# Graph network kernel, adjacency build: one 128-partition store of counts per window, or four stores of 32 partitions sent off an epoch apart

## What is computed

```python
edge_index = jnp.stack([src, dst])
h = jnp.maximum(_layernorm(x, axis=-1), 0.0)
x = x + _L0_gnn_ref(h, edge_index, ...)          # aggr = segment_sum(x[src], dst)
h = jnp.maximum(_layernorm(x, axis=-1), 0.0)
x = x + _L1_gnn_ref(h, ..., src, dst)            # the same sums, divided by the degree
...                                              # two further layers, untouched
```

## Time and profile before

| | us |
|---|---|
| median of 3 runs | 3777.47 |
| lowest, highest | 3775.76, 3778.92 |
| the profiled execution | 3770.99 |
| its span (first to last instruction) | 3769.6 |
| in it: epochs of the adjacency build | about 63 to 483 |
| in it: aggregation of the first layer | 495.4 to 639 |

### The profile page before, as it was taken

The page is one execution under the profiler, slowest core; times in us unless marked ns, Lnnn a source line. Parts: engine busy times, 40 slices in busy tenths (PEclk is TensorE's granted clock), DMA queues, the critical chain, the costliest instruction groups (busy, mean ns, idle before and its releaser), DMA issues. The chain is left out here.

```text
span 3769.6 us, 52194 instructions
## 1 busy us (share of the span) xinstructions
PE 3028.6 (80%) x16694; PEld 2344.0 (62%) x16694; DVE 2390.8 (63%) x3938; ACT 1261.2 (33%) x2681; POOL 1989.3 (53%) x2077
## 2 busy tenths in 40 slices
PE   5666689899688888888886479999888878787886
PEld 3555544455466666666664248888787577777775
DVE  7777768446698888888888656665555333333333
ACT  2334401100134344444433358777775200000000
POOL 4000000000277777777773157777777477777776
PEclk8788789899899999999998679999999989899987
DMA  3444475447344544444541145555555655555553
GB/s 133 182 200 210 189 322 229 187 185 291 91 114 114 116 117 114 110 117 116 117 110 43 67 149 217 202 216 195 194 201 190 233 194 195 195 195 194 195 194 93
DMA packets 236209, 633.91 MB, mean 168 GB/s; under 512 B 59204, under 2 KB 179506, under 8 KB 221088
## 3 DMA queue, kind: packets, MB, share of 16 engines
q1 hardware_dynamic: 170632, 494.18, 35.4%
q0 software_dynamic: 65312, 136.39, 14.0%
HBM read 412.69 MB, written 217.68 MB: 167 GB/s over the span
## 5 line engine op out<-in xcount | busy, mean ns | idle before, releaser
L1752 POOL DMA_INDIRECT edge_buffers<-rel_table,relidx x1222 | 1155.7, 946 | 459.4 <-issue 284.6
L1069 POOL DMA_INDIRECT round_buffers<-xs_t,srcs x806 | 766.2, 951 | 569.9 <-DMA xd_t<-round_buffers 324.5
L1795 PE MATMUL sums<-count_windows,H 128*128 128x208 f32 x3800 | 855.7, 362 | 30.6 <-ACT trio L1941 28.8
L1869 DVE TENSOR_TENSOR trio<-trio,sums 128x128 f32 x1242 | 356.9, 287 | 685.7 <-PE sums L1767 492.4
L1795 PEld LDWEIGHTS sums<-count_windows,H 128*128 128x128 f32 x3800 | 684.0, 203 | 47.3 <-issue 29.4
L1767 PE MATMUL sums<-edge_buffers 128*128 128x128 f32 x2340 | 372.4, 293 | 162.1 <-DMA edge_buffers<-rel_table,relidx 155.0
L1767 PEld LDWEIGHTS sums<-edge_buffers 128*128 128x128 f32 x2340 | 340.0, 202 | 190.1 <-DMA edge_buffers<-rel_table,relidx 156.1
L889 POOL IOTA trio<- 128x806 int32 x1 | 0.8, 806 | 604.0 <-ACT H L538 604.0
L1213 ACT ACTIVATE trio<-sums 128x128 f32 x806 | 223.8, 278 | 278.9 <-PE sums L1191 204.9
L1113 PE MATMUL sums<-round_buffers,ident 128*128 128x408 f32 x620 | 279.2, 534 | 30.6 <-DMA round_buffers<-xs_t,srcs 29.2
L1116 PEld LDWEIGHTS sums<-round_buffers 128*128 128x128 f32 x1612 | 243.5, 198 | 76.5 <-issue 66.1
(11 more groups left out here) (361 smaller groups left out, 4531.9 us busy)
## 6 DMA issues: line engine op xcount, KB each, us to landing
step_counts<-count_windows SPq DMA_DIRECT2D x38, 2600.0 KB, 9.2
count_windows<-step_counts SPq DMA_DIRECT2D x38, 2600.0 KB, 10.0
chunk_and_window<-adj SPq DMA_DIRECT2D x10, 5600.0 KB, 16.1
round_buffers<-xd_t SPq DMA_DIRECT2D x806, 68.0 KB
adj_chunk<-adj SPq DMA_DIRECT2D x9, 5600.0 KB, 16.6
adj<-adj_window SPq DMA_DIRECT2D x11, 3850.0 KB, 11.5
adj<-chunk_and_window SPq DMA_DIRECT2D x10, 3850.0 KB, 10.9
rel_table<-table_stages SPq DMA_DIRECT2D x50, 512.0 KB, 2.6
```

The costliest lines, as they stand in the source:

```text
L1069: nc.gpsimd.indirect_dma_start(rows[r % RING][:, k * RW:(k + 1) * RW], None, xs_t[:, :], bass.IndirectOffsetOnAxis(ap=srcs[:, t:t + 1], ax ...
L1752: nc.gpsimd.indirect_dma_start(slot(p * IG + i, k), None, rel_t[p][:, :], bass.IndirectOffsetOnAxis(ap=relidx[:, i * U + k:i * U + k + 1], ...
L1795: m = nc.tensor.matmul(pb[4][:, 0:SW * R].rearrange("p (s r) -> p s r", r=R), H[:, h, :], counts[:, w % 2, :, h * R:(h + 1) * R], start=(h ...
L1869: nc.vector.tensor_tensor(held, held, part_of(g)[:, j * P:(j + 1) * P], ALU.add).then_inc(added_n, 1)
```

## The change

SP no longer issues a window's store as one transfer of 128 partitions, but as four of 32 partitions (`PIECES_OF = 4`), with the same bytes per partition and the same total. The fourth opening matmul of each epoch now raises a new semaphore, `s_epoch_loaded`. For windows 0 to 18, piece g waits until the banks of epoch g of the next window have been opened; the pieces of the last two windows are issued one right after the other. Each piece raises `s_adj` by 16, so every wait on it is for four times the count.

```diff
+PIECES_OF = 4
...
-        root_n = sem("s_first_root")
+        root_n, eload_n = sem("s_first_root"), sem("s_epoch_loaded")
...
                 for j in range(4):
-                    nc.tensor.matmul(half[:, j * 512:j * 512 + SLOTS // 4 * CELLS], zeros[:, 0:P],
-                                     zeros[:, 0:SLOTS // 4 * CELLS], start=True, stop=False)
+                    m = nc.tensor.matmul(half[:, j * 512:j * 512 + SLOTS // 4 * CELLS], zeros[:, 0:P],
+                                         zeros[:, 0:SLOTS // 4 * CELLS], start=True, stop=False)
+                m.then_inc(eload_n, 1)
...
-                    nc.scalar.wait_ge(s_adj, 16 * (w - 1))
+                    nc.scalar.wait_ge(s_adj, 16 * PIECES_OF * (w - 1))
...
                 if w:
-                    nc.sync.wait_ge(s_adj, 16 * w)
-                nc.sync.dma_start(adj[:, bass.ds(first, SPANNED * CELLS)], filled[w % 2][:, :]).then_inc(s_adj, 16)
+                    nc.sync.wait_ge(s_adj, 16 * PIECES_OF * w)
+                n = P // PIECES_OF
+                for g in range(PIECES_OF):
+                    if w < WINDOWS - 2:
+                        nc.sync.wait_ge(eload_n, GROUP * (w + 1) + g + 1)
+                    nc.sync.dma_start(adj[g * n:(g + 1) * n, bass.ds(first, SPANNED * CELLS)],
+                                      filled[w % 2][g * n:(g + 1) * n, 0:SPANNED * CELLS]).then_inc(s_adj, 16)
```

More of the change, by code:

```diff
@@ L726, in build @@
         dsum = B1T[:, NP - DST:NP].rearrange("p (b w) -> p b w", w=WD)
-        nc.sync.wait_ge(s_adj, 16 * WINDOWS)
+        nc.sync.wait_ge(s_adj, 16 * PIECES_OF * WINDOWS)
         nc.sync.wait_ge(eout_n, EPOCHS)
```

## The result

The kernel after takes 3967.89 us (median of 4 runs, 3966.34 to 3968.74), the kernel before 3778.18 in the same comparison (4 runs): ratio 1.050, 95% interval 1.049 to 1.052. The forecast was 3816 us with a range up to 3935; the sign was right, the size was a fifth of the true one. The profiled execution took 3968.74 us, with a span of 3967.4.

A forecast was written before the change was run, and what follows sets the result against it. The prediction took PE's register loads, slowed beside each window's store, to bound the build. 3771.0 us profiled + 15 (build) + 23 (its end) = 3809; from the median, 3777.5 + 38 = 3816 us, range 3775 to 3935.

The forecast's parts named there:

- What bounds the build: Build: PE's register load, at 0.31 of its speed while a store's packets move, sets the pace; stake 78 us.
- Where a piece lands: Epoch, opening matmuls starting at T: packets move from T + 1.95, the next register load starts at T + 2.6, so they meet.
- How long a piece moves: Store of 32 partitions: 4.6 us taken, between 2.3 (engines keep their rate) and 9.2 (a quarter of the rate).
- How many pieces slow a load: PE's register loads: two of a window's four pieces taken, with four and one or none as bounds.
- price of 2.7 us per load: PE's register load: its end moves by +2.7 us beside a piece that moves for 4.6 us.
- the build's term: Build: windows of 20.8 us, +0.8 for each of the 19 windows whose pieces are spread, +15 us.
- rival (1): Build: half rate and every piece slows the load, windows of 26.8 us, 3930 us in all; chance 0.17.
- The store's own chain: SP's stores: first piece waits for the landing of the previous window's four, so no window is shorter than 20.7 us.
- rival (5): SP's waits on opened banks release nothing, as late first pieces queue up those behind; counted in the main case.
- The end of the build: Last two windows take 18.4 us each instead of 9.2, delaying two chunks by 9.2 each, window 19 about 5: +23 us.
- What costs nothing: SP's three more issues, PE's signal, the next number load on SP, ACT's wait for landings and DVE's work: no cost.
- the DMA share near 0.9: Sign in the profile after: DMA share near 0.9 over the build, with about half the GB/s at a time.

The follow-up runs named there:

- E1: The changed kernel without the waits on the opened banks, its four pieces of 32 partitions issued one right after the other: 3894.86 us, ratio 1.033.
- E2: The changed kernel with pieces cut along columns, four transfers of 128 partitions by 1925 columns, same releases: 3801.73 us, ratio 1.008.
- E3: E2 with pieces released by the closed banks of an epoch instead of the opened ones: 3703.59 us, ratio 0.982; repeat 3709.59 us, ratio 0.982.
- E4: The changed kernel with its pieces of 32 partitions released by the closed banks instead of the opened ones: 3870.88 us, ratio 1.026.
- E9: The changed kernel with two pieces of 64 partitions, released by the opened banks of the next window's first and third epoch: 3905.12 us, ratio 1.034.
- E5: The changed kernel with all four pieces read from partitions 0 to 31, counts wrong: 5014 us on a chip where the kernel before took 4788 us.
- E6: The changed kernel with all four pieces read from partitions 96 to 127, counts wrong: 4957 us on a chip where the kernel before took 4788 us.

## Why the prediction was wrong

**The account that closes.** In each profile I summed the 84 register loads' time above 1.36 us, and set the end of the build (last closing matmul) beside it:

| kernel | excess of loads, us | build ends, us | against before: excess | end |
|---|---|---|---|---|
| before | 82.6 | 483.2 | | |
| after | 265.2 | 664.0 | +182.6 | +180.9 |
| E1 | 192.1 | 592.1 | +109.5 | +108.9 |
| E2 | 111.0 | 511.1 | +28.4 | +27.9 |
| E3 | 8.5 | 408.2 | -74.1 | -75.0 |
| E4 | 168.2 | 569.3 | +85.6 | +86.1 |
| E9 | 199.1 | 600.1 | +116.5 | +116.9 |

In seven kernels the build moves by what the loads take, to within 2 us. E5 and E6 fit as well, summed the same way: excess 287.2 and 241.9, ends 687.9 and 641.0, so against before +204.6 and +204.7, and +159.3 and +157.8. No other term is needed: not SP's extra issues, not ACT's wait for landings, not DVE. Nor the lower clock by itself: PE's busy time in the build rose from 286 to 322 us at the lower clock, but a register load starts 2.4 to 2.7 us after its epoch's opening at either clock, and the next opening follows the load.

**What bounds the build: right.** The diagnosis from the earlier trace rows, a register load slowed beside the store, carries all of this, and the 78 us named as the stake were real: E3 got 68 to 75 of them.

**Where a piece lands: right.** Packets were forecast from T + 1.95, or later at the low clock, against a load at T + 2.6. In the window above the bank openings start at 331.22 and end at 333.04, SP issues at 333.21, and the load starts at 333.7. E4 against the changed kernel (97 us) and E3 against E2 (98 us) show the price of that phase directly. Here the trace decided the sign before the run.

**How long a piece moves: right, by a choice.** I took 4.6 us between 2.3 and 9.2; a landing of 6.1 us means about 4.7. The Trainium skill's page "SBUF — State Buffer", section "Door 1: The DMA port swizzle", had 8 of 16 ports for partitions 0 to 31 and for 0 to 63, and the trace agrees in both: 6.1 us for 32 partitions, 11.3 for 64, where 128 partitions by a quarter of the columns need 3.7. The stores here move at 209 GB/s by the shares above, between the 189 GB/s at 1 MiB and the limit of about 218 that the Trainium skill's table in that section gives for 8 ports. No row of the trace spoke for the middle value; only that section did.

**How many pieces slow a load: wrong, and this is the step that failed.** I took two of four, as the middle between four and one or none, with the idea that only partitions which share a way with partition 0 count. All four do: 4.45 and 4.56 us at the median beside the third and fourth piece of the changed kernel, 4.4 in E6, where only partitions 96 to 127 are read. With the forecast's own price of 2.7 us per load, four instead of two make a window 26.8 us and not 20.8, and the build's term 129 us and not 15; measured are 29.0 and 181. The rows did not support a middle: two values, "any reading" and "only the shared way", give four or two, and nothing in them spoke for the second. That DVE's load in a late stage had been slowed just like PE's beside any store that there was, was weak evidence for the first. I kept it as rival (1) with a chance of 0.17.

**The size even in rival (1): too small.** It had 26.8 us per window and 3930 us. A load hit by a piece was taken at 1.36 + 2.7 = 4.06 us; measured are 4.45 to 5.09. Two things were left out. After a wait of 3 to 4 us PE's clock is at the low level of 1.2 GHz (PEclk 0.50 from 331.10 to 332.00 above), the openings take 1.82 us and not the 1.0 of the sum, and so the packets of the piece start 0.8 us later and cover the load nearly to its end. And the speed beside a half-rate piece is lower than 0.31. The load of 5.09 us starts with the packets, at 326.1; they move for some 4.7 us, and the 0.4 left over run at full speed, so 0.96 of its 1.36 us took 4.7: 0.20. By the same working the 4.45 us beside partitions 64 to 95, with 0.3 us free ahead of the packets (333.7 to 334.0), give (1.36 - 0.3) / 4.15 = 0.26. The longest loads, covered from start to end, agree: 6.4 us is a speed of 0.21, 5.3 one of 0.26. With 4 x 3.3 = 13.2 us of excess on 16.0 the window comes to 29.2, measured 29.0.

**The store's own chain: not reached.** The floor of 20.7 us per window, and SP waiting on landings, never came to bear, because PE was slower still. (SP's slack of 9.6 us per window in the forecast counted the first window's wait of 21.5; without it 8.4.) SP's waits in the build (total us, times, longest), against the earlier trace rows:

```profile
SPq L711 <- PE sums L649: 390.3, 57, 7.4
SPq L710 <- PE sums L649: 127.6, 18, 21.5
```

57 + 18 = 75 waits of SP were for the opened banks, so the new waits did release the pieces: rival (5) is out too. In E1, without them, the last piece of the window issued from 314.5 on lands at 334.6 and the next window's first goes at 340.3, so PE is the slower one there as well.

**The end of the build: direction right, size wrong.** 23 us were forecast, 8 came. The last two windows do take twice as long to move (window 19 from 640.6 to its landing at 660.7, 20.1 us, where it was 10.7), but the last three epochs now run beside window 19's store and are slowed themselves; the end of the build moves along with the landing and covers most of it. That part is in the 181. So PE's idle before the first two chunks grew from 7.17 to 9.10 and from 2.33 to 7.27 us, not by 9 each.

**What costs nothing: right**, by the table. Of the other signs, the DMA share near 0.9 was wrong: it is 0.65, since the pieces wait for slower epochs.

## What to carry to other kernels

Look at where an engine's register load falls against the stores that read SBUF: it is no busy time of any engine, and shows only as "issue" idle and in the sequencer's own rows. Cut a transfer along the columns and keep its 128 partitions, and choose the release so that its packets fill the gap between two loads, counting 0.2 us to the issue and 0.8 us to the first packet; four pieces of the same size cost 5.0% or gain 1.8% by these two choices alone. And where two mechanisms give different counts and no row tells them apart, forecast one of them with its own number, not a middle that neither gives.

## What the hardware showed that I had not expected

A register load of PE (20 numbers) takes 1.36 us alone, and 1.36 beside copies within device memory at 247 GB/s. Beside a store that reads SBUF from 128 partitions at full rate it takes 4.37 us. Beside half-rate stores, when they cover it from start to end, it takes up to 6.4 us where partitions 0 to 63 are read and up to 5.3 where 64 to 127 are; single pieces of 32 partitions, which end about when the load does, cost 5.0 and 4.4. So reading any part of SBUF by DMA slows it about threefold and more. Halving the rate gives it little or nothing back: the speed was 0.20 to 0.26 in the workings above, against 0.31 beside the store at full rate (at best 0.37 in E9, a load of 3.71 us beside partitions 64 to 127), and the store lasts twice as long. ACT's load of four numbers is slowed in the same way, 0.31 to 1.08 us. What the load and the DMA engines share is not shown; only that it is on the reading side of SBUF and not one partition's way alone. A copy from SBUF to SBUF was not run.
